# Keeping signed gate peaks and a larger share of finished units in a quantised feed-forward kernel on Trainium2

## The chip, the cores and the metric

The program runs on one core of one Trainium2 chip. The metric is the device time of one execution in microseconds (us), and the runs of one kernel are summed up by their median. Engines are named as in the profile: PE is TensorE, ACT is ScalarE, DVE is VectorE, POOL is GpSimd and SP is SyncE, which here only issues transfers. Each engine works through its own instructions in order; a wait at the head of that queue holds everything behind it.

## What is computed

A cross-attention layer is followed by a feed-forward layer whose every intermediate tensor is rounded to 16-bit integers with one scale for the whole tensor. Only the second part is touched here:

```python
def act_qdq(x):
    qmax = 2.0 ** 15 - 1.0
    scale = jnp.maximum(jnp.max(jnp.abs(x)) / qmax, 1e-12)
    return jnp.clip(jnp.round(x / scale), -qmax - 1.0, qmax) * scale
...
x = act_qdq(x)
up = act_qdq(x @ lpbq_dequant(w_up).T)
gate = act_qdq(x @ lpbq_dequant(w_gate).T)
sig = fixed_qdq_u16(jax.nn.sigmoid(gate))
gate = act_qdq(gate * sig)
o = act_qdq(gate * up)
return o @ lpbq_dequant(w_down).T
```

x has 8192 rows of 512 values, the inner width is 1536. Each act_qdq needs the largest magnitude of its whole tensor before a single value can be rounded. So gate * sig can't be rounded before all of it has been seen once, and o can't be rounded before all products have been seen once.

## The kernel before

The attention part (function opening) ends at 643 us and leaves the normalised rows. The function feed does the rest. It cuts the rows into 16 blocks of 512 and each block's 1536 columns into three units of 128 x 2048 values: 48 units in all (NU). The stages are these.

**Gate pass.** For every block PE multiplies with the gate weights; two halves per unit go from PSUM to a slot of ff_raw (evict, line 1635, ACT). DVE takes the largest magnitude of the unit (raw_peak, line 1417), and POOL stores the unit to DRAM (store_raw, line 1331). ff_raw has three slots. Beside it the up and down weights are quantised.

**Up pass.** PE multiplies the same blocks with the up weights, 48 steps of two halves again; one step is called a stage here, numbered 0 to 47. Each stage takes PE 10.36 us. The block of integers that a PE block needs is loaded by SP (load_hq, line 1206) and split by DVE into two f16 parts (split, line 1406) at the start of every stage 3j+1, for the block that begins with stage 3j+3. While PE works, the gate is finished in two steps.

- A first step (first, lines 1500 and 1655) loads a gate unit, makes its integers, their magnitudes, the sigmoid and its integers, and the largest product of the two. Which units a stage takes is set by first_units (line 1076): 7 in four stages. The integers of all but the last KEPT units are stored to DRAM; those KEPT units stay in SBUF.
- When all 48 largest products are known, a second step (second, lines 1508 and 1667) makes the rounded gate from the integers: a sigmoid on ACT, its integers on DVE, and the product with the scale on DVE. READY units get it, two per stage from stage SECOND = 48 - READY/2 on. In a stage with second steps DVE does the first one, the stage's raw_peak, and the second one, in this order. The first KEPT second steps work on the units that were kept. The rest load their integers again: refill w (load_again, line 1226, SP) brings unit w for second step v = KEPT + w into one of nine slots (AR = 9). The first nine refills find empty slots; a later one waits until the store of the second step that used the slot before has landed. POOL issues that store (store_gated, line 1341) one stage later in its queue, behind the raw store of the stage.

SP's order in the up pass is, for each stage: load_hq if the stage is 3j, the loads of gate units, and from SECOND on a wait for the peak of the stage before and two refills:

```python
for n in range(NU):
    if n % UNITS == 0:
        load_hq(n // UNITS + 1)
    for u in first_units(n):
        load_gate(u + GR)
    if n >= SECOND:
        sp.wait_ge(m["peak"], NU + n - 1)
        load_again(2 * (n - SECOND))
        load_again(2 * (n - SECOND) + 1)
```

**Late stage.** With the scale of the up values known, ACT makes the magnitude of each up unit (line 1720) and DVE the largest product of it with the gate's magnitude (line 1575), 48 places in the order that the tables order, made and home give (lines 952 to 968). PE has nothing to do. A "late" unit, one of the 48 - READY that no second step reached, gets its sigmoid (L1707), integers (L1497), product (L1559) and magnitude (L1727) here. A finished unit needs its magnitude only: on ACT (L1724, "act"), on DVE (L1566 and L1568, "dve"), or already in the up pass (L1681, "done"). Gate units that are not in SBUF are loaded by POOL (load_gated, line 1348), up units by SP (load_up, line 1237). The first loads into the "wq" slots that belong to late units are issued early, in the up pass (soon, line 1359).

**Down stage.** Both factors are loaded once more, multiplied and rounded (last_up, line 1729, ACT; last_product, line 1538, DVE), and PE multiplies with the down weights.

Of the kernel before, what the change touches and what calls it, by code (L numbers as in the profile page):

```python
# [17 lines left out]
P = 128  # L18
# [19 lines left out]
READY = 36  # L38
EARLY = 4
XR = 9  # L40
KEPT = 8
# [870 lines left out]
def feed_memory(s, keep):  # L912
# [8 lines left out]
    for n in ("red_w", "all_w", "unit_w", *(f"{a}_{b}" for a in "gpuo" for b in ("red", "all"))):  # L921
        mem[n] = s.sb(n, [P, 1], F32)
    return mem


def feed(nc, keep, mem, hT_d, hq_d, gate_d, up_d, gate_q, x1_d, out, NB, scale_d, mats):
# [19 lines left out]
    WQ, NEAR = 4, 7  # L946
# [54 lines left out]
    with Scope(nc, "fd") as s:  # L1001
        t_gin, t_ring, t_sig, t_sq, ab, hq, t_h, raw = (mem[n] for n in ("gin", "ring", "sig", "sq", "ab", "hq", "h_parts", "raw"))
# [13 lines left out]
        def floats(t):  # L1016
# [4 lines left out]
        hb = [floats(ab[:, :, :])[:, 0, :], t_gin[:, GR - 1, :]]  # L1021
# [18 lines left out]
                  for n in ("gate_all", "up_all"))  # L1040
# [17 lines left out]
        m = s.sems("g_red g_all p_red p_all u_red u_all o_red o_all dve g_scales u_scales o_scales "  # L1058
                   "hq ah al mm out peak w_peak w_red w_all w_scales w_sent w_q w_real w_hi w_lo "
                   "gq_act gq_dve ab sig sq gpeak g2 mag gp neg ga_late ga_act ga_dve ua prod "  # L1060
                   "fsig fsq fgp fgq fuq fo foq foh fol fmm y")
        gpk, gpk_v, gpk_p = whole_peak(nc, mem, m, "g", keep["gate_peak"][:, :])
# [13 lines left out]
        def first_units(n):  # L1076

            return [u for u in range(NU) if 4 * (u // 7) + u % 7 // 2 == n]
# [9 lines left out]
        def kept(j):  # L1088

            return spare[:, j, :] if j < 6 else more[:, j - 6, :]  # L1090
# [16 lines left out]
        def have_gq(eng, u):  # L1107

            if u % 3 == 0:
                eng.wait_ge(m["gq_act"], u // 3 + 1)  # L1110
            else:
                eng.wait_ge(m["gq_dve"], u - u // 3)
# [26 lines left out]
        def gated(i):  # L1139

            kind, j = g_slot[i][0] if home[i] == "load" else ("unit", order[i])
            if kind == "wq":
                return hq[:, j, :] if j < 2 else ab[:, j - 2, :]
# [37 lines left out]
        with nc.Block() as block:  # L1181
            @block.sync
            def _(sp):
# [30 lines left out]
                def load_gate(u):  # L1214
                    if u < NU:
# [4 lines left out]
                        else:  # L1220
                            have_gq(sp, u - GR)
                            sp.wait_ge(m["ab"], u - GR + 1)
# [3 lines left out]
                def load_again(w):  # L1226
                    if w < AGAIN:
                        if w < AR:
                            sp.wait_ge(m["sig"], NU)
                            sp.wait_ge(m["ab"], NU)  # L1230
# [95 lines left out]
            def _(pool):  # L1326
# [21 lines left out]
                def load_gated(i):  # L1348
# [3 lines left out]
                    if kind == "wq" and prior < 0:  # L1352
                        pool.wait_ge(m["al"], 2 * NB)
                        pool.wait_ge(m["gpeak"], NU)
# [15 lines left out]
                gpk_p(pool)  # L1370
                for n in range(NU):
                    if n == SECOND:
# [30 lines left out]
            def _(dve):  # L1403
# [13 lines left out]
                def raw_peak(n):  # L1417
# [465 lines left out]
```

## Time and profile before

| | us |
|---|---|
| median of 3 runs | 2347.43 |
| lowest and highest run | 2347.32, 2349.02 |
| span of the profiled execution, first to last instruction | 2347.3 |
| attention part | 0 to 643 |
| gate and up pass | 643 to 1644 |
| late stage, with the scales ahead and the first down unit behind it | 1644 to 1837 |
| down stage | 1837 to 2347 |

The page gives the profiled execution's own time as its span; nothing is reported around it. Busy shares of the span are PE 86%, DVE 73%, ACT 60% and POOL 29%, but the stages differ, so they are to be read stage by stage. A busy PE is one that has matmuls in hand. In the rows a line number is that of the kernel before.

### The profile page before, as it was taken

The numbers are of one execution on the slowest core, as the hardware profiler recorded it, in microseconds if no ns is written. First come the engines' busy times: TensorE is split into PE (matmuls) and PEld (weight loads), VectorE is DVE, ScalarE is ACT, GpSimd is POOL, SyncE is SP. The second block draws the span as 40 slices with busy tenths as digits, with TensorE's granted clock in tenths as the row PEclk, the third lists the DMA queues.
The fourth block names the chain that finished last, engine by engine and source line by source line (L and its number), as shares of the span: only waits on it lengthen the run. The fifth ranks groups of instructions, "written<-read, shape, count | busy, mean of one in ns | idle before, by whom it ended". The sixth has DMA issues, their size and how long they took to land.

```text
span 2347.3 us, 25386 instructions
## 1 busy us (share of the span) xinstructions
PE 2020.4 (86%) x9524; PEld 945.0 (40%) x9524; DVE 1715.7 (73%) x1387; ACT 1398.2 (60%) x1599; POOL 670.6 (29%) x662
## 2 busy tenths in 40 slices
PE   5888888888599999999999999999000699999998
PEld 2444444444244444444444444444000344444443
DVE  8799999999634534532499998999899644577641
ACT  4678887887422322322499996676899633366530
POOL 2599999998300000000121110222111000000000
PEclk9999999999799999999999999999555899999999
DMA  7789999998346656743699995787998755555541
GB/s 297 283 314 337 348 337 346 335 350 316 126 181 226 225 207 223 259 148 144 242 378 390 378 369 209 264 320 293 401 419 327 291 229 208 205 201 232 233 152 72
DMA packets 131162, 634.60 MB, mean 270 GB/s; under 512 B 12256, under 2 KB 12768, under 8 KB 91104
## 3 DMA queue, kind: packets, MB, share of 16 engines
q1 hardware_dynamic: 85888, 316.81, 37.0%
q0 software_dynamic: 45152, 316.16, 34.6%
q8 instruction: 76, 1.25, 0.2%
q14 instruction: 46, 0.38, 0.0%
HBM read 430.69 MB, written 202.24 MB: 270 GB/s over the span
## 4 chain that ended last, share of the span: by engine, by line
PE 64%; issue 3%; DVE 3%; ACT 2%; POOL 0%; DVEq 0%; ACTq 0%; POOLq 0%
PE fd_pp L1777 42%; PE fd_pp L1791 21%; ACT ff_ring L1720 1%; DVE ff_sig L1575 1%; DVE ff_h_parts L1559 1%; DVE ff_sq L1497 1%; ACT ff_sig L1707 0%; DVE ff_sq L1566 0%; DVE kept_gate L1568 0%; DVE ff_gin L1510 0%; DVE ff_hq L1549 0%; ACT ff_hq L1632 0%; ACT ff_ring L1746 0%; ACT ff_sig L1736 0%; DVE kept_o_peak L1575 0%
## 5 line engine op out<-in xcount | busy, mean ns | idle before, releaser
L1791 PE MATMUL fd_pp<-ff_down,kept_gate 128*128 128x512 f16 x1536 | 458.9, 381 | 193.1 <-DVE ff_up L1616 193.1
L1777 PE MATMUL fd_pp<-ff_h_parts,kept_gate 128*128 128x512 f16 x2304 | 499.6, 380 | 14.3 <-DVE ff_h_parts L1415 14.3
L1777 PE MATMUL fd_pp<-ff_h_parts,ff_up 128*128 128x512 f16 x2304 | 497.4, 379 | 0.0
L1639 ACT ACTIVATE ff_raw<-fd_pp 128x1024 f32<-128x1024 f32 x192 | 194.3, 1017 | 396.5 <-PE fd_pp L1777 396.5
L1777 PEld LDWEIGHTS fd_pp<-ff_h_parts,kept_gate 128*128 128x128 f16 x2304 | 225.9, 98 | 287.9 <-DVE ff_h_parts L1415 14.7
L1777 PEld LDWEIGHTS fd_pp<-ff_h_parts,ff_up 128*128 128x128 f16 x2304 | 225.4, 98 | 271.8
L1420 DVE TENSOR_REDUCE kept_gate_peak<-ff_raw 128x1 f32<-128x2048 f32 x48 | 109.7, 2285 | 292.9 <-ACT ff_raw L1639 292.9
L1791 PEld LDWEIGHTS fd_pp<-ff_down,kept_gate 128*128 128x128 f16 x1536 | 150.6, 98 | 375.9 <-issue 195.8
L1791 PE MATMUL fd_pp<-ff_down,ff_up 128*128 128x512 f16 x768 | 292.2, 380 | 0.0
L1746 ACT ACTIVATE ff_ring<-ff_hq,kept_g 128x2048 int16<-128x2048 f32 x48 | 96.0, 1999 | 191.1 <-DVE ff_hq L1549 189.7
L790 PE MATMUL at_psO<-kept_wo,at_ahi 128*128 128x512 f16 x512 | 155.5, 386 | 36.2 <-ACT at_alo L277 31.6
L1614 DVE CAST kept_gate<-ff_ring 128x2048 f16<-128x2048 int16 x48 | 33.3, 693 | 180.1 <-PE fd_pp L1791 136.7
L790 PE MATMUL at_psQ<-kept_wq,at_xhi 128*128 128x512 f16 x512 | 155.5, 386 | 4.8 <-ACT at_xlo L268 1.6
L1334 POOL DMA_DIRECT2D gate_scratch<-ff_raw x48 | 26.5, 553 | 463.3 <-DVE kept_gate_peak L1420 463.3
L697 POOL TENSOR_TENSOR at_kv_rows<-at_kv_rows 128x1024 f32<-128x1024 f32 x62 | 146.8, 2368 | 4.9
L515 DVE TENSOR_TENSOR at_kv_rows<-at_kv_rows,at_psQ 128x2048 f32<-128x2048 f32 x64 | 143.3, 2279 | 4.4 <-PE at_psQ L790 4.4
L1394 POOL DMA_DIRECT2D out<-ff_h_parts x15 | 12.5, 834 | 467.3 <-DVE ff_h_parts L1592 440.0
L520 DVE TENSOR_REDUCE at_sc<-at_kv_rows 128x64 f32<-128x2048 f32 x64 | 143.0, 2274 | 0.0
L1497 DVE TENSOR_SCALAR ff_sq<-ff_sig 128x2048 uint16<-128x2048 f32 x96 | 117.3, 1222 | 9.8 <-ACT ff_sig L1665 6.0
L1420 DVE TENSOR_REDUCE kept_up_peak<-ff_raw 128x1 f32<-128x2048 f32 x48 | 109.5, 2282 | 18.3 <-ACT ff_raw L1639 17.9
L1334 POOL DMA_DIRECT2D up_scratch<-ff_raw x48 | 41.2, 859 | 249.0 <-DVE kept_up_peak L1420 249.0
L1791 PEld LDWEIGHTS fd_pp<-ff_down,ff_up 128*128 128x128 f16 x768 | 75.4, 98 | 91.4 <-issue 1.4
(239 smaller groups left out, 3454.9 us busy)
## 6 DMA issues: line engine op xcount, KB each, us to landing
ff_raw<-up_scratch SPq DMA_DIRECT2D x66, 1024.0 KB, 8.5
gate_scratch<-ff_raw POOLq DMA_DIRECT2D x48, 1024.0 KB, 9.1
ff_gin<-gate_scratch SPq DMA_DIRECT2D x48, 1024.0 KB, 8.7
up_scratch<-ff_raw POOLq DMA_DIRECT2D x48, 1024.0 KB, 7.7
ff_gin<-gate_integers SPq DMA_DIRECT2D x73, 512.0 KB, 5.8
gate_integers<-ff_ring POOLq DMA_DIRECT2D x43, 512.0 KB, 8.7
ff_up<-up_scratch SPq DMA_DIRECT2D x21, 1024.0 KB, 9.5
kept_xs<-in_x SPq DMA_DIRECT2D x32, 512.0 KB, 14.6
```

The costliest lines, as they stand in the source:

```text
L515: nc.vector.tensor_tensor(keys, keys, psQ[t % 2][:, :].unsqueeze(1).to_broadcast([P, W, D]), ALU.mult).then_inc(m["prod"], 1)
L520: nc.vector.tensor_reduce(raw[:, t % 2], kv[:, t % KR, :, 0:D].rearrange("p w (h e) -> p w h e", h=H), AX.X, ALU.add).then_inc(m["raw"], 1)
L697: nc.gpsimd.tensor_tensor(lower, lower, upper, ALU.add).then_inc(m["half"], 1)
L790: mm = nc.tensor.matmul(out[:, :], a[:, slot, c, :], w[b][:, c, :], start=(q == 0), stop=(q == len(todo) - 1))
L1334: pool.dma_start(to[n // UNITS, n % UNITS], raw[:, n % UNITS, :]).then_inc(stored[n % UNITS], 16)
L1420: nc.vector.tensor_reduce(keep[to][:, k:k + 1], raw[:, n % UNITS, :], AX.X, ALU.max, apply_absolute_value=True).then_inc(m["peak"], 1)
L1497: nc.vector.tensor_scalar(sq[:, :], sig[:, a, :], 65536.0, 65535.0, ALU.mult, ALU.min).then_inc(m["sq"], 1)
L1614: nc.vector.tensor_copy(piece(oh, k), fo_oq).then_inc(m["foh"], 1)
L1639: nc.scalar.activation(raw[:, n % UNITS, h * 2 * BLK:(h + 1) * 2 * BLK], pp[(2 * n + h) % 4][:, :, :].rearrange("p a t -> p (a t)"), ACT.C ...
L1746: nc.scalar.activation(fo_oq, fo_o, ACT.Copy, scale=g[:, 13:14]).then_inc(m["foq"], 1)
L1777: mm = nc.tensor.matmul(pp[k % 4][:, h, :], wt[w][:, c, f:f + P], a[:, b % 2, :, c, :], start=(q == 0), stop=(q == len(todo) - 1))
L1791: mm = nc.tensor.matmul(pp[k % 8 // 2][:, k % 2, :], a[b % 2][:, f, t * P:(t + 1) * P], wt[w][:, f, :], start=(q == 0 and i == 0), stop=(q ...
```

## The change

READY goes from 36 to 42 and KEPT from 8 to 10, so that SECOND moves from stage 30 to 27, and AWAY, the first kept unit, from 40 to 38. The two kept units more lie in two slots added to ring; the buffer ab is gone.

In the gate pass DVE takes each unit's maximum and minimum in place of its largest magnitude; the last unit of the gate pass and of the up pass is reduced in two halves. The scales of the gate are used negated, so the gate integers are negated, and the largest product of a first step is taken from the signed integers (the negative gates, whose negated integers are positive); the positive side is covered by one value, the product at the largest gate, made once from a 128 x 1 column. The first step's magnitude on ACT and the integers on DVE go away: ACT makes all integers. A slot of ring is now free for a new unit when the first step's largest product is taken, where it was the sigmoid. First steps run 15 in eight stages, where it was 7 in four. SP's first refills wait for the end of the first steps, and POOL's early list has two slots to look at in place of four. ACT's first two conversions of the down stage (last_up) wait for the last use of the two kept slots that they write, and no longer for every kept slot from there on.

```diff
-READY = 36
+READY = 42
...
-KEPT = 8
+KEPT = 10
...
-    mem = {"gin": s.sb("gin", [P, 4, UE], F32), "ring": s.sb("ring", [P, 4, UE], I16),
+    mem = {"gin": s.sb("gin", [P, 4, UE], F32), "ring": s.sb("ring", [P, 6, UE], I16),
...
-           "ab": s.sb("ab", [P, 2, UE], I16), "hq": s.sb("hq", [P, 2, DC * BLK], I16),
+           "hq": s.sb("hq", [P, 2, DC * BLK], I16),
...
-    WQ, NEAR = 4, 7
+    WQ, NEAR = 2, 7
...
-            return [u for u in range(NU) if 4 * (u // 7) + u % 7 // 2 == n]
+            return [u for u in range(NU) if u // 15 * 8 + u % 15 * 8 // 15 == n]
...
-            return spare[:, j, :] if j < 6 else more[:, j - 6, :]
+            return spare[:, j, :] if j < 6 else more[:, j - 6, :] if j < 8 else ring[:, QR + j - 8, :]
...
-                eng.wait_ge(m["sig"], u - QR + 1)
+                eng.wait_ge(m["gpeak"], u - QR + 1)
...
-                    if n == SECOND:
+                    if n == SECOND - 1:
                         ppk_p(pool)
...
-                def raw_peak(n):
-                    dve.wait_ge(m["out"], 2 * n + 2)
-                    to, k = ("gate_peak", n) if n < NU else ("up_peak", n - NU)
-                    nc.vector.tensor_reduce(keep[to][:, k:k + 1], raw[:, n % UNITS, :], AX.X, ALU.max,
-                                            apply_absolute_value=True).then_inc(m["peak"], 1)
...
+                def gate_range(n):
+                    for h in halves(n):
+                        values, k = part(n, h), n + h
+                        nc.vector.tensor_reduce(keep["gate_top"][:, k:k + 1], values, AX.X, ALU.max)
+                        last = nc.vector.tensor_reduce(keep["gate_low"][:, k:k + 1], values, AX.X, ALU.min)
+                    last.then_inc(m["peak"], 1)
+
+                def up_range(n):
+                    for h in halves(NU + n):
+                        values, k = part(NU + n, h), n + h
+                        last = nc.vector.tensor_reduce(keep["up_peak"][:, k:k + 1], values, AX.X, ALU.max, apply_absolute_value=True)
+                    last.then_inc(m["peak"], 1)
...
                 def first(u):
                     sigmoid_integer(u, u % 2)
-                    gate_integers(u + 2)
-                    dve.wait_ge(m["ab"], u + 1)
-                    nc.vector.tensor_tensor_reduce(out=sig[:, u % 2, :], in0=ab[:, u % 2, :], in1=sq[:, :], scale=1.0,
+                    nc.vector.tensor_tensor_reduce(out=sig[:, u % 2, :], in0=integers(u), in1=sq[:, :], scale=1.0,
...
-                    if u % 3 == 0:
-                        gq_free(act, u)
-                        if u >= AWAY:
-                            act.wait_ge(m["mm"], NB * PAIRS)
-                        nc.scalar.activation(integers(u), gin[:, u % GR, :], ACT.Copy, scale=g[:, 5:6]).then_inc(m["gq_act"], 1)
+                    gq_free(act, u)
+                    if u >= AWAY:
+                        act.wait_ge(m["mm"], NB * PAIRS)
+                    nc.scalar.activation(integers(u), gin[:, u % GR, :], ACT.Copy, scale=g[:, 5:6]).then_inc(m["gq"], 1)
                     need(act, m["gpeak"], u - 1)
-                    nc.scalar.activation(ab[:, u % 2, :], gin[:, u % GR, :], ACT.Abs, scale=g[:, 5:6]).then_inc(m["ab"], 1)
...
-                            act.wait_ge(m["prod"], max(g_last["unit", u] for u in range(AWAY + 6, NU)) + 1)
+                            act.wait_ge(m["prod"], max(g_last["unit", u] for u in range(AWAY + 6, AWAY + 8)) + 1)
```

Two places show how instructions stand against each other. The first is DVE's queue before the split of stage 43 (L1413 or L1417, the CAST from ff_hq). L1510 or L1538 is the end of a second step, L1497 or L1527 its sigmoid integers, L1420 or L1442 the peak of a stage. Before, from second step 22, the first one of stage 41:

```order
L1510 SCALAR_TENSOR_TENSOR ff_gin<-ff_sq,kept_g,ff_gin 128x2048
L1420 TENSOR_REDUCE kept_up_peak<-ff_raw 128x1
L1497 TENSOR_SCALAR ff_sq<-ff_sig 128x2048
L1510 SCALAR_TENSOR_TENSOR ff_gin<-ff_sq,kept_g,ff_gin 128x2048
L1497 TENSOR_SCALAR ff_sq<-ff_sig 128x2048
L1510 SCALAR_TENSOR_TENSOR ff_gin<-ff_sq,kept_g,ff_gin 128x2048
L1420 TENSOR_REDUCE kept_up_peak<-ff_raw 128x1
L1497 TENSOR_SCALAR ff_sq<-ff_sig 128x2048
L1510 SCALAR_TENSOR_TENSOR ff_ring<-ff_sq,kept_g,ff_ring 128x2048
L1413 CAST ff_h_parts<-ff_hq 128x2048
L1415 TENSOR_TENSOR ff_h_parts<-ff_hq,ff_h_parts 128x2048
```

Those were second steps 22 to 25. Now, from second step 30, the first one of stage 42:

```order
L1538 SCALAR_TENSOR_TENSOR ff_gin<-ff_sq,kept_g,ff_gin 128x2048
L1442 TENSOR_REDUCE ff_up_peak<-ff_raw 128x1
L1527 TENSOR_SCALAR ff_sq<-ff_sig 128x2048
L1538 SCALAR_TENSOR_TENSOR ff_gin<-ff_sq,kept_g,ff_gin 128x2048
L1417 CAST ff_h_parts<-ff_hq 128x2048
L1419 TENSOR_TENSOR ff_h_parts<-ff_hq,ff_h_parts 128x2048
```

The split follows the second steps of stage 42 in both; steps 30 and 31 stand where 24 and 25 stood.

The second place is SP's queue at stages 39 to 42: six refills and the load of integers that the split of stage 43 needs. Each refill waits for the semaphore of its slot, w mod 9; the names are those of an earlier scope (at_q_lo is slot 0, at_scaled 1, at_turned 2, at_taken 3, at_rest 4, at_out 5, at_kv_ready 6, at_kv_out 7, at_consts 8), and at_sqe or at_hT_sb is the peak of the stage before. Before, refills 18 to 23:

```order
L1235 DMA ff_gin<-gate_integers 128x2048 [waits at_q_lo,at_sqe]
L1235 DMA ff_gin<-gate_integers 128x2048 [waits at_scaled]
L1235 DMA ff_gin<-gate_integers 128x2048 [waits at_turned,at_sqe]
L1235 DMA ff_gin<-gate_integers 128x2048 [waits at_taken]
L1235 DMA ff_gin<-gate_integers 128x2048 [waits at_rest,at_sqe]
L1235 DMA ff_gin<-gate_integers 128x2048 [waits at_out]
L1212 DMA ff_hq<-h_integers 128x2048 [waits at_ssq_v]
```

Now, refills 24 to 29:

```order
L1239 DMA ff_gin<-gate_integers 128x2048 [waits at_kv_ready,at_hT_sb]
L1239 DMA ff_gin<-gate_integers 128x2048 [waits at_kv_out]
L1239 DMA ff_ring<-gate_integers 128x2048 [waits at_consts,at_hT_sb]
L1239 DMA ff_gin<-gate_integers 128x2048 [waits at_q_lo]
L1239 DMA ff_gin<-gate_integers 128x2048 [waits at_scaled,at_hT_sb]
L1239 DMA ff_gin<-gate_integers 128x2048 [waits at_turned]
L1217 DMA ff_hq<-h_integers 128x2048 [waits at_x_ssq]
```

The load of integers still follows the second refill of stage 41; that refill is number 29 now, and waits for slot 2, where it was number 23 and slot 5.

## Rows read from the trace of the kernel before

**Rows 1.** Stretches: length, busy PE, PEld, DVE, ACT, POOL, PE clock, DMA share, GB/s.

```profile
642.00:1145.00 503.00, 498.14 (x2299) 225.40 (x2300) 197.29 (x121) 138.29 (x119) 35.26 (x65) 0.99 0.58 202
1460.00:1644.00 184.00, 183.71 (x852) 83.08 (x849) 171.98 (x102) 122.07 (x83) 44.05 (x54) 1.00 0.78 291
1643.80:1836.80 193.00, 0.00 (x0) 0.00 (x1) 175.41 (x156) 177.09 (x94) 20.46 (x34) 0.51 0.92 373
```

**Rows 2.** The chain of waits, in order of time: start, length, engine, tile, line.

```profile
646.86 996.86 PE fd_pp L1777 x4608
...
1836.83 497.62 PE fd_pp L1791 x2292
```

**Rows 3.** Stretches: the late stage from its first magnitude to its last product.

```profile
1652.80:1827.30 174.50, 0.00 (x0) 0.00 (x0) 163.23 (x136) 162.79 (x86) 17.38 (x28) 0.50 0.94 384
```

**Rows 4.** Instructions by form, one form of each line: total busy us, mean ns.

```profile
L1724 ACT ACTIVATE kept_gate<-kept_gate 128x2048 int16<-128x2048 int16 x5 | 9.5, 1894 | 0.0
...
L1559 DVE TENSOR_TENSOR ff_h_parts<-ff_sig,ff_sq 128x2048 f32<-128x2048 int16 x3 | 6.9, 2293 | 0.1
...
L1727 ACT ACTIVATE ff_hq<-ff_h_parts,kept_g 128x2048 int16<-128x2048 f32 x3 | 6.0, 2002 | 2.6 <-DVE ff_h_parts L1559 2.6
...
L1707 ACT ACTIVATE ff_sig<-ff_hq,kept_g 128x2048 f32<-128x2048 int16 x3 | 6.0, 1992 | 0.0
...
L1568 DVE TENSOR_TENSOR ff_gin<-ff_gin,ff_sq 128x2048 int16<-128x2048 int16 x3 | 3.7, 1225 | 0.1
```

**Rows 5.** DVE in order of time, stages 41 to 44 of the up pass.

```profile
1582.64 2.29 DVE L1420 TENSOR_REDUCE kept_up_peak<-ff_raw 128x1 f32<-128x2048 f32 x1
...
1593.00 2.29 DVE L1420 TENSOR_REDUCE kept_up_peak<-ff_raw 128x1 f32<-128x2048 f32 x1 [0.84 <-ACT ff_raw L1639]
1595.20 1.22 DVE L1497 TENSOR_SCALAR ff_sq<-ff_sig 128x2048 uint16<-128x2048 f32 x1
...
1598.73 0.69 DVE L1413 CAST ff_h_parts<-ff_hq 128x2048 f16<-128x2048 int16 x1
...
1604.11 2.28 DVE L1420 TENSOR_REDUCE kept_up_peak<-ff_raw 128x1 f32<-128x2048 f32 x1
...
1613.72 2.29 DVE L1420 TENSOR_REDUCE kept_up_peak<-ff_raw 128x1 f32<-128x2048 f32 x1
```

**Rows 6.** POOL in order of time, its stores after the peak of stage 41.

```profile
1585.22 0.96 POOL L1334 DMA_DIRECT2D up_scratch<-ff_raw  x1 [4.94 <-DVE kept_up_peak L1420]
1586.17 0.53 POOL L1346 DMA_DIRECT2D gate_integers<-ff_gin  x1
```

**Rows 7.** SP in order of time, the second refill of stage 41 and load_hq.

```profile
1591.61 0.32 SPq L1235 DMA_DIRECT2D ff_gin<-gate_integers  x1
1591.97 0.44 SPq L1212 DMA_DIRECT2D ff_hq<-h_integers  x1
```

**Rows 8.** Lines L1212 (load_hq, 3) and L1346 (store_gated, 17), 1500 to 1600 us.

```profile
DMA to landing us min/median/max: 4.3/4.5/4.6
...
DMA to landing us min/median/max: 3.9/5.2/6.7
```

**Rows 9.** All engines in order of time, the end of the late stage.

```profile
1827.37 3.89 ACT L1736 ACTIVATE ff_sig<-ff_raw,kept_g 128x2048 int16<-128x2048 f32 x2 [4.89 <-DVE kept_o_peak L1575]
...
1829.40 2.29 DVE L1549 TENSOR_TENSOR ff_hq<-ff_gin,ff_sig 128x2048 f32<-128x2048 int16 x1 [1.89 <-ACT ff_sig L1736]
1831.61 0.21 DVE L905 TENSOR_SCALAR kept_g<-ff_o_all,kept_g 128x1 f32<-128x1 f32 x1
```

**Rows 10.** DMA issues of the late stage, gate loads: count, KB, median us to landing.

```profile
kept_gate<-gate_integers POOLq DMA_DIRECT2D x10, 512.0 KB, 8.6
```

**Rows 11.** Stretches: the late stage's first part, and the up pass's first part.

```profile
1652.80:1750.00 97.20, 0.00 (x0) 0.00 (x0) 91.37 (x75) 91.55 (x49) 10.70 (x17) 0.50 1.01 418
1230.00:1260.00 30.00, 30.00 (x140) 13.62 (x139) 29.58 (x24) 28.41 (x19) 4.82 (x8) 1.00 1.01 406
1200.00:1400.00 200.00, 200.00 (x928) 90.69 (x927) 196.97 (x156) 182.70 (x116) 36.54 (x50) 1.00 0.98 380
```

More of the change, by code:

```diff
@@ L916, in feed_memory @@
         keep[n] = [keep[n + "_all"][:, i] for i in range(2)]
[L917 removed]
+    mem = {"gin": s.sb("gin", [P, 4, UE], F32), "ring": s.sb("ring", [P, 6, UE], I16),
            "sig": s.sb("sig", [P, 3, UE], F32), "sq": s.sb("sq", [P, UE], U16),
[L919 removed]
+           "hq": s.sb("hq", [P, 2, DC * BLK], I16),
            "h_parts": s.sb("h_parts", [P, 2, 2, SUB, DC, P], F16), "raw": s.sb("raw", [P, UNITS, UE], F32)}
[L921 removed]
+    for n in ("red_w", "all_w", "unit_w", *(f"{a}_{b}" for a in "puo" for b in ("red", "all"))):
         mem[n] = s.sb(n, [P, 1], F32)
+    for n in ("g_red", "g_all"):
+        mem[n] = s.sb(n, [P, 2], F32)
+    for n in ("gate_top", "gate_low", "up_peak", "gated_peak"):
+        keep[n] = s.sb(n, [P, count + 1], F32)
+    keep["o_peak"] = s.sb("o_peak", [P, count], F32)
+    mem["top_sig"] = s.sb("top_sig", [P, 1], F32)
+    mem["top_int"], mem["top_sq"] = s.sb("top_int", [P, 1], I16), s.sb("top_sq", [P, 1], U16)
     return mem
@@ L1001, in feed @@
     with Scope(nc, "fd") as s:
-        t_gin, t_ring, t_sig, t_sq, ab, hq, t_h, raw = (mem[n] for n in ("gin", "ring", "sig", "sq", "ab", "hq", "h_parts", "raw"))
+        t_gin, t_ring, t_sig, t_sq, hq, t_h, raw = (mem[n] for n in ("gin", "ring", "sig", "sq", "hq", "h_parts", "raw"))
+        top_sig, top_int, top_sq = (mem[n] for n in ("top_sig", "top_int", "top_sq"))
         red, allm, unit = (mem[n] for n in ("red_w", "all_w", "unit_w"))
@@ L1415, in split, with halves, part @@
                     nc.vector.tensor_tensor(lo, hq[:, b % 2, :], hi, ALU.subtract).then_inc(m["al"], 1)
-                def raw_peak(n):
-                    dve.wait_ge(m["out"], 2 * n + 2)
-                    to, k = ("gate_peak", n) if n < NU else ("up_peak", n - NU)
-                    nc.vector.tensor_reduce(keep[to][:, k:k + 1], raw[:, n % UNITS, :], AX.X, ALU.max,
-                                            apply_absolute_value=True).then_inc(m["peak"], 1)
+                def halves(n):
+                    return (0, 1) if n % NU == NU - 1 else (0,)
+                def part(n, h):
+                    if n % NU < NU - 1:
+                        dve.wait_ge(m["out"], 2 * n + 2)
+                        return raw[:, n % UNITS, :]
+                    dve.wait_ge(m["out"], 2 * n + h + 1)
+                    return raw[:, n % UNITS, h * 2 * BLK:(h + 1) * 2 * BLK]
+                def gate_range(n):
[9 more added lines that the diff above has]
+                    last.then_inc(m["peak"], 1)
                 def weight_peak(i, h):
@@ new lines, in top_product @@
+                def top_product():
+                    dve.wait_ge(m["top_s"], 1)
+                    nc.vector.tensor_scalar(top_sq[:, :], top_sig[:, :], 65536.0, 65535.0, ALU.mult, ALU.min).then_inc(m["top_q"], 1)
+                    dve.wait_ge(m["top_q"], 1)
+                    nc.vector.scalar_tensor_tensor(out=keep["gated_peak"][:, NU:NU + 1], in0=top_int[:, :], scalar=-1.0,
+                                                   in1=top_sq[:, :], op0=ALU.mult, op1=ALU.mult).then_inc(m["top_p"], 1)
```

68 lines of the change are left out of this document (35 added, 33 removed).

## The prediction

> **What bounds the kernel now.** I read the profile by stretches first. In the gate pass and the up pass TensorE (PE) works without a gap: the chain of waits is one PE piece of 996.9 us, and the down stage is another of 497.6 us [rows 2]. Between them lies the late stage, 193 us in which PE does nothing while ScalarE (ACT) and VectorE (DVE) finish the 12 units that the up pass left over and form all 48 products [rows 1]. From the first magnitude to the last product it is 174.5 us, ACT busy for 162.8 and DVE for 163.2 [rows 3]; their records overlap the next one a little, so both queues are full. So there are two ways to change the time: the late stage is paid in full, and in the up pass nothing costs until DVE or ACT falls behind PE. DVE is near that: in the second part of the up pass it is busy for 172.0 of 184 us [rows 1].
>
> **Late stage: -18 us.** Late units go from 12 to 6; finished units whose magnitude ACT takes here go from 15 to 18, those where DVE takes it from 8 to 9 (the table that lines 952 to 968 of the kernel before make, worked out with the new numbers). A late unit costs ACT a sigmoid of 1.99 us and a magnitude of 2.00, and DVE an integer step of 1.22 and a product of 2.29; an ACT magnitude of a finished unit is 1.89 and DVE's pair for one is 1.23 plus a shorter negation [rows 4, 5]. ACT: 6 x 3.99 - 3 x 1.89 = 18.3 us less. DVE: 6 x 3.51 = 21.1 less, and about 1.9 more for the pair: 19.2. I take 18. The upper bound is 20, both queues with some idle time gone. The lower bound is 14: two early gate loads vanish (with two "wq" slots, both first users are finished units, so the list of early loads is empty), and the first late unit, at place 7, is now loaded only after the first product. Such a load took 8.6 us to land, in the median of ten [rows 10]; issued some 4.4 us into the stage it lands at 13, where ACT wants it after four magnitudes, at 7.6; DVE has four products to form meanwhile, so of these 5.4 us at most 4 are lost.
>
> **Tail of the late stage: -1.9 us.** The first down-stage factor (last_up(0)) waited for the last product: ACT idle 4.89 us, then 1.99 us, and DVE's 2.29 us behind it before the last quantiser [rows 9]. Now it waits for place 38 and is made long before. DVE's multiply follows the last product at once, its 2.29 us still cover POOL's reduction, and the quantiser starts 1.9 us earlier. Bounds 0 and 1.9.
>
> **Up pass, second part: +28 us.** This is the term that decides. A second step v may write its result over a slot of nine, and SP refills that slot when the store of the earlier occupant has landed. The refill w waits for the store of second step v = KEPT + w - 9. That was w - 1; with KEPT = 10 it is w + 1. SP's second refill of stage 41 was w = 23 and waited for v = 22, the first second step of stage 41; now it is w = 29 and waits for v = 30, the first one of stage 42. SP is in order, and right behind that refill stands the load of the next integer block (load_hq), which DVE's split at the start of stage 43 needs.
>
> The trace has the whole chain, one stage earlier. DVE starts the peak of stage 41 at 1582.64 [rows 5]; POOL issues the raw store at 1585.22 and only then the store of v = 22, at 1586.17 [rows 6]; that has landed at 1591.61, when SP refills, and SP issues load_hq at 1591.97 [rows 7]: 9.33 us from the start of the peak. The load takes 4.5 us [rows 8]: 13.83. DVE reaches the split 5.73 us after the start of the peak of stage 42 (1593.00 to 1598.73) [rows 5]. Today the load lands at about 1596.5, 2.3 us ahead. After the change the same chain hangs on the peak of stage 42 itself, so the split starts 13.83 us after it instead of 5.73: DVE stands still for 8.1 us, with every later peak and second step queued behind it.
>
> It happens wherever SP ends a stage 3j-1 with such a refill (w of 9 and more, up to 31): before the splits of stages 34, 37, 40 and 43, four times. Nothing of DVE's work can fill the hole, since the queue is in order. Of slack there is little: a stage with a split takes DVE 11.11 us when it runs without waits (1593.00 to 1604.11), one without 9.61 (to 1613.72), so three take 30.33 against 3 x 10.36 = 31.08 of PE: 0.75 us per block, and 0.75 per stage in the last two. So 4 x (8.1 - 0.75) - 1.5 = 27.9 us later at the end of the pass. PE waits for the splits too: the last one ends 13.83 + 1.86 us after the start of a peak that is by then 3 x 7.35 us late, 1593.0 + 22.1 + 15.7 = 1630.8, where PE would begin its last block at 1643.7 - 31.1 = 1612.6 [rows 2]. That is 18 us, of which the two blocks before take 3 and 7; but DVE is later still, so the pass ends by DVE. The peak of the last stage in two halves would give up to 1.1 us if DVE were waiting there; it isn't any more, so 0.
>
> For the store and the load the Trainium skill (DMA: Bandwidth & Descriptors, Anatomy of one DMA) has a fit of about 2.0 us plus bytes over 436 GB/s, 3.2 us for such a half MB. By that the chain would be 7.1 + 3.2 us, the hole 4.6 and the term +14, and the sum would be a gain of 6 us. The trace disagrees: the store took 5.4 us here, 5.2 in the median, 3.9 at the least, and the load 4.3 to 4.6 [rows 8]. I go by the trace. Its ends: 3.9 and 4.3 make 7.8 + 4.3 = 12.1, a hole of 6.4 and a term of 21; 6.7 and 4.6 make 15.2, 9.5 and 33.5.
>
> **Costed at nothing.** Gate pass: a minimum beside each maximum, 48 x 2.29 = 110 us more on DVE, which was busy for 197 of 503 us there [rows 1]; so 306 us were idle. Where weight work falls into the same stage and the two don't fit into 10.36 us, the slot of ff_raw comes free later; there are three, and the cost stays 0 while the delay is under two stages, 20 us. First part of the up pass: ACT loses 48 magnitudes and takes over DVE's 32 conversions, so both have less to do; DVE was the tight one there, 29.6 of 30 us [rows 11]. Both are hidden by PE; only the earlier end of the part counts, and the new table of first units spends it. The extra one-column steps between the passes, five or six of 0.2 us, are covered by the missing magnitude of the first unit, some 2 us of ACT like its others [rows 4], and by the three pairs that PE may run ahead, 15.5 us.
>
> **Sum.** The profiled execution has a span of 2347.3 us, the median of the runs is 2347.43: the same within 0.1. 2347.3 + 27.9 - 18.0 - 1.9 = **2355.3 us**, slower by 0.34%. A change of under 0.2%, 4.7 us, is what a measurement can't tell from none.
>
> **Rivals.**
> **No hole: 2327.4 us.** If load_hq is issued within 1.2 us of the start of the stage's peak, it lands before DVE's split and only -18 - 1.9 is left. For it: today's split never waits there, and the integers are loaded a whole block ahead on paper. Against it: the load that SP issues at 1591.97 follows a store that POOL can't issue before the peak [rows 6, 7], and I find no other path. It decides where the chain is under 5.73 us; break-even with the savings is at a hole of 6.1 us. Chance 0.13.
> **Quick landings: 2346.4 us, no change.** While DVE stands still fewer transfers are under way, and all four stores and loads land as fast as the fastest row: +21 - 20 - 1.9 = -0.9. Against it: the 17 stores and 3 loads of that stretch lie about their medians although the DMA engines are not full there. Chance 0.08. The fit of the Trainium skill, above, lies beyond it.
> **DMA full in the first part: about 2364 us.** 15 first units in 8 stages need 15 x 1.57 + 8 x 1.05 + 2.7 x 0.52 = 33.4 MB in 82.9 us, 403 GB/s, where 14 needed 384. The stretch moved 380 on average at a share of 0.98, and 406 in one of 30 us [rows 11]. If 380 were the limit, the part would run 5 us late per 8 stages for 20 stages, 12.5 us, of which PE's lead hides some 4: 8 us on top. Against it: the late stage moved 418 GB/s for 97 us [rows 11]. Chance 0.07. The Trainium skill (DMA: Bandwidth & Descriptors, Specifications) gives 358 GB/s of HBM per core, by which even the present part could not run; that trace row decides against it.
>
> **Chances and range.** Forecast with its bounds 0.72, the rivals 0.13, 0.08, 0.07. The forecast's ends: +21.1 - 20 - 1.9 = 2346.5 and +33.5 - 14 = 2366.8. The range 2345 to 2367 leaves out the first rival and a little at the top. Faster by over 0.2%: the first rival and a bit of the second, 0.14. Within: the rest of the second and the low end of the forecast, 0.12. Slower: 0.74.
>
> **What would show it.** DVE's CAST of the split (L1417) waits for the DMA of ff_hq four times, some 8 us each, from stage 34 on; PE has three gaps in the up pass, about 18 us together; the first magnitude of the late stage starts at about 1681 instead of 1652.8; the late stage has 6 late products and takes about 156 us from first magnitude to last product; the first last_up of ACT starts before the last product. Wrong if that CAST does not wait, if PE's up pass has no gap, or if gaps lie before stage 27.

## The result, and the profile after

The changed kernel takes 2369.81 us (median of 4 runs, 2368.63 to 2371.02); the kernel before, on the same chip, 2348.22 us. The ratio is 1.0093, with a 95% interval of 1.0080 to 1.0105: **slower by 21.6 us**. The prediction was 2355.3 us, slower by 8, in a range of 2345 to 2367. The sign and the mechanism of the loss were right; the size was not, and the measured time lies above the range. Two terms carry the miss, the saving in the late stage above all.

The span of the profiled execution is 2369.2 us, where it was 2347.3. The stretches of the changed kernel that answer to [rows 1, 3], with the same columns (length, busy PE, PEld, DVE, ACT, POOL, PE clock, DMA share, GB/s):

```profile
642.00:1145.00 503.00, 497.94 (x2298) 225.36 (x2299) 302.63 (x170) 137.71 (x119) 35.28 (x65) 0.99 0.57 201
1460.00:1676.00 216.00, 190.27 (x852) 84.34 (x850) 172.94 (x100) 127.53 (x86) 44.15 (x54) 0.96 0.65 244
1685.60:1720.00 34.40, 0.00 (x0) 0.00 (x0) 22.11 (x19) 24.44 (x13) 2.11 (x4) 0.50 1.00 399
1720.00:1790.00 70.00, 0.00 (x0) 0.00 (x0) 64.91 (x57) 64.10 (x35) 7.74 (x13) 0.50 1.01 417
1685.60:1852.40 166.80, 0.00 (x0) 0.00 (x0) 144.37 (x126) 149.96 (x80) 15.57 (x27) 0.50 0.97 397
```

The gate pass carries its 105 us of extra DVE work beside an unchanged PE. The second part of the up pass has the same DVE work as before, 172.9 us, in a longer time. The late stage has less work (ACT 150.0 us where it was 162.8), but takes 166.8 us, and in its first 34 us neither engine is busy for more than 24.4.

The chain of waits answers to [rows 2]. Its first piece of PE now ends at 1514, and the holes follow: stretches in which DVE stands still ahead of a split, because the block of integers has not landed. The PE piece, and the chain at the second of the four holes (start, length, what):

```profile
647.06 867.34 PE fd_pp L1810 x4008
...
1538.76 2.21 DVE ff_up_peak L1442
1540.97 0.28 issue
1541.25 0.95 POOL up_scratch L1338
1542.20 6.28 DMA gate_integers<-ff_ring
1548.50 0.32 SPq L1239
...
1548.86 5.15 DMA ff_hq<-h_integers
1554.03 0.70 DVE ff_h_parts L1417
```

This is the chain of the prediction, link by link: peak, POOL's raw store, the landing of the second step's store, SP's refill, the block load, the split. It takes 15.27 us from the start of the peak where 13.83 were predicted. The splits of DVE and the gaps of PE, each in order of time, with the wait ahead in brackets:

```profile
1514.41 0.69 DVE L1417 CAST ff_h_parts<-ff_hq 128x2048 f16<-128x2048 int16 x1 [8.67 <-PE fd_pp L1810]
...
1554.03 0.69 DVE L1417 CAST ff_h_parts<-ff_hq 128x2048 f16<-128x2048 int16 x1 [9.55 <-DMA ff_hq<-h_integers]
...
1594.23 0.69 DVE L1417 CAST ff_h_parts<-ff_hq 128x2048 f16<-128x2048 int16 x1 [10.13 <-DMA ff_hq<-h_integers]
```

```profile
1556.04 32.83 PE L1810 MATMUL fd_pp<-ff_h_parts,ff_up 128*128 128x512 f16 x144 [5.40 <-DVE ff_h_parts L1419]
1596.24 33.20 PE L1810 MATMUL fd_pp<-ff_h_parts,ff_up 128*128 128x512 f16 x144 [7.37 <-DVE ff_h_parts L1419]
1636.42 33.59 PE L1810 MATMUL fd_pp<-ff_h_parts,ff_up 128*128 128x512 f16 x144 [6.97 <-DVE ff_h_parts L1419]
```

The first hole is put down to PE, since the split also waits for matmuls; but its block load was issued at 1509.1 and such loads took 5.1 to 5.4 us here, so it landed when the split began. (In the kernel with the early gate loads, below, whose up pass has the same order, the same hole is put down to the block load.) The list of waits for 1400 to 1680 us gives the other three 29.8 us together:

```profile
DVE ff_h_parts L1417 <- DMA ff_hq<-h_integers: 29.8, 3, 10.1
PE fd_pp L1810 <- DVE ff_h_parts L1419: 19.7, 3, 7.4
```

So there are four holes of 38.5 us in all, where 32.4 were predicted, and three gaps of PE, 19.7 us, where 18 were. The start of the late stage, ACT and POOL in order of time:

```profile
1685.63 5.79 ACT L1753 ACTIVATE ff_ring<-ff_raw,kept_g 128x2048 int16<-128x2048 f32 x3 [7.50 <-DVE kept_g L1567]
...
1690.36 0.53 POOL L1360 DMA_DIRECT2D ff_ring<-gate_integers  x1 [4.77 <-DVE ff_o_peak L1607]
...
1695.34 1.91 ACT L1757 ACTIVATE ff_hq<-ff_hq 128x2048 int16<-128x2048 int16 x1 [2.03 <-DMA ff_hq<-gate_integers]
...
1702.73 2.00 ACT L1740 ACTIVATE ff_sig<-ff_ring,kept_g 128x2048 f32<-128x2048 int16 x1 [5.48 <-DMA ff_ring<-gate_integers]
...
1706.65 2.29 DVE L1607 CUSTOM_DVE_ANT_0 ff_sig<-ff_hq,ff_ring 128x2048 bf16<-128x2048 int16 x1 [9.96 <-ACT ff_ring L1753]
```

The gate load of the first late unit (place 7) is issued at 1690.36, after the first product, and ACT can go on at 1702.73: 12.4 us. ACT waits 5.5 us for it, and DVE 10 us behind ACT.

The end of the late stage answers to [rows 9]:

```profile
1849.60 3.88 ACT L1769 ACTIVATE ff_sig<-ff_raw,kept_g 128x2048 int16<-128x2048 f32 x2
...
1850.11 2.29 DVE L1607 CUSTOM_DVE_ANT_0 ff_sig<-ff_ring 128x2048 bf16<-128x2048 int16 x1
...
1852.55 2.28 DVE L1581 TENSOR_TENSOR ff_hq<-ff_gin,ff_sig 128x2048 f32<-128x2048 int16 x1
...
1860.30 1.01 PE L1824 MATMUL fd_pp<-ff_down,kept_gate 128*128 128x512 f16 x2 [190.29 <-DVE ff_up L1648]
```

Where the time went: the first magnitude starts at 1685.63 where it was 1652.82, **+32.8**; from there to the end of the last product 166.8 where it was 174.5, **-7.7**; from there to PE 7.9 where it was 9.6, **-1.7**; the down stage **-1.6**. That is the 21.9 us between the spans. The last of these is not explained by the change: over the ten kernels of this document the down stage takes 508.9 to 510.5 us.

### The profile page after: what moved, and what is told of

It reads as the page before. It is cut to its first block, busy times and chain, and to the rows that moved or that the text cites. A ratio compares the mean times of both kernels' runs of the same rounds, so it can differ in the third digit from the quotient of the medians.

```text
span 2369.2 us, 25333 instructions
## 1 busy us (share of the span) xinstructions
PE 2025.4 (85%) x9524; PEld 945.8 (40%) x9524; DVE 1765.6 (75%) x1404; ACT 1348.9 (57%) x1571; POOL 663.4 (28%) x664
## 4 chain that ended last, share of the span: by engine, by line
PE 58%; DVE 6%; DMA 4%; issue 3%; ACT 2%; POOL 0%; SPq 0%; DVEq 0%; ACTq 0%; POOLq 0%
PE fd_pp L1810 37%; PE fd_pp L1824 21%; DVE ff_gin L1538 2%; DVE ff_sq L1527 1%; ACT ff_ring L1753 1%; DMA gate_integers<-ff_gin 1%; DMA ff_ring<-gate_integers 1%; DMA ff_hq<-h_integers 1%; DVE ff_sig L1607 1%; DVE ff_up_peak L1442 0%; DMA kept_gate<-gate_integers 0%; DMA ff_hq<-gate_integers 0%; DVE ff_ring L1538 0%; DVE ff_h_parts L1591 0%; DMA gate_integers<-ff_ring 0%
## 5 line engine op out<-in xcount | busy, mean ns | idle before, releaser
L1810 PE MATMUL fd_pp<-ff_h_parts,ff_up 128*128 128x512 f16 x2304 | 503.8, 382 | 19.7 <-DVE ff_h_parts L1419 19.7
L1435 DVE TENSOR_REDUCE ff_gate_top<-ff_raw 128x1 f32<-128x2048 f32 (+1 forms) x49 | 109.9, 2242 | 187.7 <-ACT ff_raw L1671 187.7
L1527 DVE TENSOR_SCALAR ff_sq<-ff_sig 128x2048 uint16<-128x2048 f32 x96 | 117.3, 1222 | 21.9 <-ACT ff_sig L1695 19.1
L1442 DVE TENSOR_REDUCE ff_up_peak<-ff_raw 128x1 f32<-128x2048 f32 (+1 forms) x49 | 109.6, 2237 | 16.1 <-ACT ff_raw L1671 15.9
L525 DVE TENSOR_TENSOR at_kv_rows<-at_kv_rows,at_pr 128x1536 f32<-128x1536 f32 x64 | 109.8, 1755 | 1.1
```

The costliest lines, as they stand in the source:

```text
L525: nc.vector.tensor_tensor(values, values, pr[:, t % 2, 0:W - 1].unsqueeze(3).to_broadcast([P, W - 1, H, HD]), ALU.mult).then_inc(m["pv"], 1)
L1435: nc.vector.tensor_reduce(keep["gate_top"][:, k:k + 1], values, AX.X, ALU.max)
L1442: last = nc.vector.tensor_reduce(keep["up_peak"][:, k:k + 1], values, AX.X, ALU.max, apply_absolute_value=True)
L1527: nc.vector.tensor_scalar(sq[:, :], sig[:, a, :], 65536.0, 65535.0, ALU.mult, ALU.min).then_inc(m["sq"], 1)
L1810: mm = nc.tensor.matmul(pp[k % 4][:, h, :], wt[w][:, c, f:f + P], a[:, b % 2, :, c, :], start=(q == 0), stop=(q == len(todo) - 1))
```

## The experiments

Theory 1: the holes come from the integer load that stands in SP's queue behind a refill, which waits for a second step two later than before. Rival: four more second steps are too much for DVE. Theory A: the late stage gives back its gain because the first late unit's gate load is no longer early. Theory B: it gives it back because its bytes are the bound. The kernel before was run again beside each group of experiments, 2348.08 us beside the first four below and 2348.48 beside the other four; the ratios are to these.

**The block load ahead of the refills.**

```
-                    if n % UNITS == 0:
-                        load_hq(n // UNITS + 1)
+                    if n % UNITS == 2:
+                        load_hq(n // UNITS + 2)
```

(Block 1 is loaded ahead of the loop.)

> The change, but SP issues the load of an integer block one stage earlier, ahead of the two refills of stage 3j-1 and no longer behind them. Theory (the refill that waits for the first second step of the stage holds the block load up): DVE's CAST of the split no longer waits for the load, PE's three gaps in the up pass (5.4, 7.4, 7.0 us) are gone, and the late stage's first magnitude starts at about 1653 in place of 1685.6. The late stage itself stays at some 167 us. Time 2369.8 - 32.8 = about 2337. Rival (42 second steps are by themselves more than DVE can do beside PE): the CAST doesn't wait, but peaks and second steps run late by themselves; the first magnitude stays behind 1670 and the time above 2354.

Measured: 2343.11 us, ratio to the kernel before 0.9978 (0.9969 to 0.9988). PE has no gap in the up pass any more, and the first magnitude starts at 1652.56, 33.1 us earlier:

```profile
1399.82 244.49 PE L1811 MATMUL fd_pp<-ff_h_parts,ff_up 128*128 128x512 f16 x1132
...
1652.56 5.79 ACT L1754 ACTIVATE ff_ring<-ff_raw,kept_g 128x2048 int16<-128x2048 f32 x3 [3.60 <-DVE kept_g L1568]
...
1667.59 1.91 ACT L1758 ACTIVATE ff_hq<-ff_hq 128x2048 int16<-128x2048 int16 x1 [7.35 <-DMA ff_hq<-gate_integers]
1675.14 2.00 ACT L1741 ACTIVATE ff_sig<-ff_ring,kept_g 128x2048 f32<-128x2048 int16 x1 [5.63 <-DMA ff_ring<-gate_integers]
```

For the up pass theory 1 holds to half a microsecond, and the rival falls. The time is 6 us above the expected one, since some of the 33 are lost again: the late stage takes 171.4 us in place of 166.8. The gate loads that POOL issues at 1651.38 and 1657.29 now run beside the first up loads, which SP began to issue at 1644.46; ACT gets them at 1667.59 and 1675.14, 16 and 18 us after their issue. In the changed kernel the holes had held DVE back: the first gate load followed the first up load by 14 us (1670.17 to 1684.45), where it is 7 us here. That this makes the difference was not tried by itself.

**The wait alone, in the kernel before.**

```
-                    if n % UNITS == 0:
+                    if n < SECOND and n % UNITS == 0:
                         load_hq(n // UNITS + 1)
...
                         load_again(2 * (n - SECOND) + 1)
+                    if n >= SECOND and n % UNITS == 0:
+                        load_hq(n // UNITS + 1)
```

> The kernel before with one part of the change's timing alone: from stage 30 on, the load of an integer block stands behind the two refills of stage 3j, one stage later than before, so that it hangs on the first second step of that stage as in the changed kernel. Theory: three holes on DVE ahead of the splits of stages 37, 40 and 43 (refills wait only from number 9 on and end with number 27), each about 9.9 us as measured in the changed kernel, less 0.75 us of slack per block and 1.5 us at the end: 3 x 9.15 - 1.5 = 26 us, time about 2374. With the 8.1 us of the prediction it would be 20.5, about 2369. Rival (the loss comes from the larger number of second steps): under 5 us, below 2353.

Measured: 2371.27 us, ratio 1.0097 (1.0080 to 1.0114), 23.2 us more than before. The three splits:

```profile
1545.68 0.69 DVE L1415 CAST ff_h_parts<-ff_hq 128x2048 f16<-128x2048 int16 x1 [8.66 <-PE fd_pp L1779]
1586.32 0.69 DVE L1415 CAST ff_h_parts<-ff_hq 128x2048 f16<-128x2048 int16 x1 [10.58 <-DMA ff_hq<-h_integers]
1624.66 0.69 DVE L1415 CAST ff_h_parts<-ff_hq 128x2048 f16<-128x2048 int16 x1 [8.28 <-DMA ff_hq<-h_integers]
```

27.5 us of holes less 3 x 0.75 and 1.5 us of slack are 23.8; the first magnitude is 23.0 us later (1675.82). The block load moved by two places in SP's queue, with nothing else of the change, costs as much as the whole change.

**The store of the second step ahead of the raw store.**

```
+                    for v in second_units(n - 1)[:1]:
+                        store_gated(v)
                     if n >= 1:
                         store_raw(NU + n - 1)
-                    for v in second_units(n - 1):
+                    for v in second_units(n - 1)[1:]:
                         store_gated(v)
```

> The change, but POOL stores the result of a stage's first second step ahead of the stage's raw store; the order of loads stays. Theory (the hole is a chain from the peak through POOL's raw store, the store of the second step, the refill and the block load): the chain starts when the second step ends, not when the peak has ended and the raw store is issued, which is 2.29 + 0.29 + 0.95 = 3.5 us earlier, so each of the four holes is about 3.5 us shorter: 14 us in all, about 2356. If the store also lands faster because no 1 MB store stands in front of it in POOL's queue (4 us in place of 6.3 to 6.6), up to 6 us each: 24 us, about 2346. Rival (the DMA engines are the limit there and the landing moves with the traffic): less than 5 us, above 2365.

Measured: 2358.27 us, ratio 1.0039 (1.0025 to 1.0053), 11.5 us less than the change, somewhat short of the 14 that the theory gave for the earlier start alone. The holes are 6.60, 6.62, 5.89 and 7.57 us, 26.7 in all. The chain of waits at the second one, to be compared with the one above:

```profile
1535.94 0.28 issue
1536.22 2.94 DMA gate_integers<-ff_ring
1539.17 0.32 SPq L1239
1539.53 8.71 DMA ff_hq<-h_integers
1548.27 0.70 DVE ff_h_parts L1419
```

The store now lands in 2.94 us where it took 6.28, and the load takes 8.71 us where it took 5.15: 11.65 and 11.43 together. What one gained the other lost, and the 1 MB raw store that stood ahead of the store is now issued at 1538.41, 1.1 us ahead of the load. The other three holes give 3.84 and 8.70, 3.03 and 7.87, 3.60 and 8.98, together 10.9 to 12.6; the other two whole chains of the change, 6.59 and 5.42, 6.65 and 5.33, give 12.0 each. Only the earlier start of the chain is left, about 3 us per hole.

For a half MB store the Trainium skill's fit (DMA: Bandwidth & Descriptors, Anatomy of one DMA — SWDGE (gpsimd) path), which is for transfers issued by POOL, gives an estimate of 3.2 us. The store that has nothing right ahead of it in POOL's queue, at 2.94 to 3.84 us here, comes near that, and the same store behind the raw store in the changed kernel, at 6.28 to 6.65, doesn't.

**The gate load of the first late unit early.**

```
-    g_slot, g_last = assign({**{("wq", j): -1 for j in range(WQ)}, **residents}, loaded)
+    soon = [loaded[0], made.index("late")]
+    g_slot, g_last = assign({**{("wq", j): -1 for j in range(WQ)}, **residents}, soon + [i for i in loaded if i not in soon])
...
-                soon = [i for i in loaded[:WQ] if late(order[i])]
```

> The change, but the two slots for early gate loads go to places 4 and 7 (the first late unit) in place of 4 and 6, and both loads are issued in the up pass at stage 46. Theory A (the late stage's start is lost because the first late unit's gate load is issued only after the first product): ACT's first late sigmoid no longer waits 5.5 us for its load nor DVE 10 us behind it; the late stage takes 158 to 161 us in place of 166.8, time about 2362 to 2364. Theory B (the late stage is bound by its bytes, 66.2 MB at 418 GB/s): only the 1 MB that moves ahead of the stage is saved, 2.5 us, about 2367.

Measured: 2363.56 us, ratio 1.0071 (1.0054 to 1.0088), 6.3 us less than the change. Neither wait at the start is there any more, and the late stage takes 161.7 us, 5.1 less. That is near theory A's 158 to 161; but with two gate loads issued ahead the stage also moves fewer bytes, 65.3 MB where it moved 66.2, and by theory B 2.2 of the 5.1 us could be theirs. The two shares were not separated, and 161.7 is not yet the 156 of the prediction.

The order of the up pass up to stage 46 is that of the change, and its splits show how much the holes vary from one execution to another:

```profile
1513.93 0.69 DVE L1417 CAST ff_h_parts<-ff_hq 128x2048 f16<-128x2048 int16 x1 [8.47 <-DMA ff_hq<-h_integers]
...
1553.24 0.69 DVE L1417 CAST ff_h_parts<-ff_hq 128x2048 f16<-128x2048 int16 x1 [9.24 <-DMA ff_hq<-h_integers]
...
1591.67 0.69 DVE L1417 CAST ff_h_parts<-ff_hq 128x2048 f16<-128x2048 int16 x1 [8.38 <-DMA ff_hq<-h_integers]
...
1630.35 0.69 DVE L1417 CAST ff_h_parts<-ff_hq 128x2048 f16<-128x2048 int16 x1 [8.62 <-DMA ff_hq<-h_integers]
...
1681.56 5.79 ACT L1753 ACTIVATE ff_ring<-ff_raw,kept_g 128x2048 int16<-128x2048 f32 x3 [7.50 <-DVE kept_g L1567]
```

They make 34.7 us where the change had 38.5, and the first magnitude starts 28.7 us later than in the kernel before, not 32.8. In the chains the store takes 5.44 to 6.42 us and the load 4.42 to 5.05, together 10.3 to 11.1. So 4.1 of the 8.1 us between the two spans lie in the up pass, where the edit does nothing before stage 46; why is not shown.

**Both repairs.** The edits are those of the first and the fourth kernel above.

> The change with both repairs: the block load ahead of the refills, and the gate loads of places 4 and 7 issued in the up pass. Theory (two independent losses): first magnitude at about 1652.6 as with the first repair alone, and of the 13 us (7.4 and 5.6) that ACT then waited for gate loads at the start of the late stage some 8 to 10 go; time about 2333 to 2335. The load of place 6 is still issued only after the first product and may hold DVE for up to 4 us: then 2337. Rival (the late stage is bound by its bytes): 2.5 us saved, 2340.6.

Measured: **2330.74 us**, ratio 0.9924 (0.9908 to 0.9941): the fastest kernel here that loads everything, 17.7 us under the kernel before and 39 under the change, and 2 us under what was expected. The first magnitude starts at 1651.19, the late stage takes 162.0 us.

**Both repairs, with fewer bytes.** Every second place of the late stage loads half of its up unit, so that part of the largest product is taken of stale values.

```
+                    w = UE // 2 if i % 2 else UE
-                    sp.dma_start(u_slot(i), up_d[u // UNITS, u % UNITS])...
+                    sp.dma_start(u_slot(i)[:, 0:w], up_d[u // UNITS, u % UNITS][:, 0:w])...
```

> As the kernel with both repairs, but of the up units that the late stage loads from DRAM every second place loads only half of its columns, so that the largest product there is taken of partly stale values; some 11 of 66 MB are left out and no work of ACT or DVE. Theory B (with the early loads in place, what keeps the late stage at 162 us is its bytes, 66 MB at 418 GB/s = 158 us, where ACT is busy for 151): the late stage falls to 152 to 155 us and the time by 7 to 10 us against the kernel with both repairs. Rival (the order of ACT and DVE and their waits for each other set it): the late stage stays above 159 us, less than 3 us saved.

Measured: 2326.91 us, ratio 0.9910 (0.9894 to 0.9927), 3.8 us less than with both repairs, where 7 to 10 were expected. In the profiled executions the spans differ by 5.2 us, and the late stage takes 155.8 us where it took 162.0, just above the 152 to 155 that theory B gave. Its stretches, first with all bytes, then with fewer:

```profile
1652.50:1687.00 34.50, 0.00 (x0) 0.00 (x0) 30.99 (x27) 30.91 (x17) 3.73 (x7) 0.50 1.01 421
1687.00:1722.00 35.00, 0.00 (x0) 0.00 (x0) 29.96 (x28) 30.44 (x17) 3.07 (x5) 0.50 1.02 419
1722.00:1757.00 35.00, 0.00 (x0) 0.00 (x0) 33.39 (x28) 33.04 (x18) 3.60 (x6) 0.50 1.02 420
1757.00:1792.00 35.00, 0.00 (x0) 0.00 (x0) 31.87 (x31) 34.75 (x20) 5.18 (x9) 0.50 1.02 418
```

```profile
1687.00:1722.00 35.00, 0.00 (x0) 0.00 (x0) 32.77 (x29) 31.89 (x17) 3.53 (x6) 0.50 0.93 350
1722.00:1757.00 35.00, 0.00 (x0) 0.00 (x0) 34.20 (x32) 34.71 (x19) 4.27 (x8) 0.50 0.90 343
1757.00:1792.00 35.00, 0.00 (x0) 0.00 (x0) 32.39 (x29) 34.75 (x20) 4.52 (x8) 0.50 0.85 333
```

The list of waits agrees: with all bytes ACT waits four times for a late unit's gate load, 7 us in all; with fewer once, 0.2 us. So the bytes do hold the stage up, but by less than theory B gave: 4 us by the medians and 6 by the two traces. With all bytes the rows show 418 to 421 GB/s at a share of 1.01 to 1.02 while ACT and DVE are not full.

**KEPT back at 8.** The only edit is `KEPT = 8`; still 42 finished units.

> The change with KEPT back at 8 alone: 42 finished units, 34 refills, and refill w waits for the store of second step w-1 as before the change. SP's order is the changed kernel's. Theory (the hole comes from the two kept units more, which let each refill wait for a second step two later): DVE's CAST of the split doesn't wait for its load, PE has no gap, and the first magnitude starts at about 1653; the late stage is that of the first repair alone (171 us, no early gate load of a late unit) with two gate loads more, 1 MB, 2.5 us: about 2343 to 2346. Rival (the four second steps more in the up pass, by themselves, make the hole): it stays, about 2366 to 2372.

Measured: 2347.78 us, ratio 0.9999 (0.9989 to 1.0008). No split waits for its load, and the first magnitude starts at 1650.45, earlier than before: the holes came with the two kept units more, not with the second steps. The late stage, though, takes 176.5 us, 2.0 more than in the kernel before, with half its late units, and the time is 2 us above the expected range. ACT waits 7.56 and 5.64 us for gate loads at its start, as with the block load moved:

```profile
1665.69 1.91 ACT L1757 ACTIVATE ff_hq<-ff_hq 128x2048 int16<-128x2048 int16 x1 [7.56 <-DMA ff_hq<-gate_integers]
1673.23 2.00 ACT L1740 ACTIVATE ff_sig<-ff_sig,kept_g 128x2048 f32<-128x2048 int16 x1 [5.64 <-DMA ff_sig<-gate_integers]
```

**KEPT back at 8, three early gate loads.** One of the two slots that this frees becomes a third "wq" slot, and the loads of places 4, 6 and 7 are issued in the up pass.

```
-    WQ, NEAR = 2, 7
+    WQ, NEAR = 3, 7
-                return hq[:, j, :]
+                return hq[:, j, :] if j < 2 else ring[:, QR, :]
-                soon = [i for i in loaded[:WQ] if late(order[i])]
+                soon = loaded[:WQ]
```

> KEPT back at 8 as in the run before, and the slot that this frees is a third one for early gate loads: those of places 4, 6 and 7 are issued in the up pass. Theory: no hole and no wait for gate loads at the start of the late stage, which takes 159 to 163 us: about 2331 to 2335, the fastest of all. Rival (bytes): 3 loads fewer in the late stage, 1.5 MB, 3.8 us under the run with KEPT at 8 alone.

Measured: 2337.25 us, ratio 0.9953 (0.9937 to 0.9970), 2 us above the expected range and not the fastest. The waits at the start are gone, and the late stage takes 166.3 us, 10 less than with KEPT at 8 alone, but 4 more than with both repairs. Against both repairs two gate loads more are needed and one more is early, so the stage moves 66.7 MB where it moved 66.2, 1.3 us at 418 GB/s; what the rest is was not tried.

## Why the prediction was right in sign and wrong in size

**Second part of the up pass: +27.9 predicted, +32.8 measured.** Mechanism, number of holes, their places and the arithmetic held: each hole is the chain less 5.73 us (15.27 - 5.73 = 9.54; 9.55 in the row), and 38.5 less 4 x 0.75 and 1.5 are 34.0. What was too small is the chain's 13.83 us, in which the store has 5.4 and the load 4.5: in the three chains that the trace of the change shows whole, the store took 6.28, 6.59 and 6.65 and the load 5.15, 5.42 and 5.33. The bounds, 21 to 33.5, held it.

Two things bear on the size of this miss. The trace before had this chain three times, at 9.5, 10.3 and 9.3 us from the start of the peak to the issue of the block load, and the prediction took the shortest; the longest is

```profile
1551.56 2.29 DVE L1420 TENSOR_REDUCE kept_up_peak<-ff_raw 128x1 f32<-128x2048 f32 x1
...
1561.88 0.57 SPq L1212 DMA_DIRECT2D ff_hq<-h_integers  x1
```

And the kernel with the early gate loads shows +28.7 with the same order, so the size is not known better than to some 4 us. The kernel with the store first shows that the two landings trade against each other at about the same sum, so the sum is the thing to price; it was 9.9 us in the prediction and 10.2 to 12.5 in the nine whole chains of the three kernels with this order. Why it came out longer is not shown. The fit of the Trainium skill that the prediction tried on both transfers is one for transfers issued by POOL, as said above; the block load is issued by SP, and none here landed in less than 4.4 us.

**Late stage: -18 predicted, -7.7 measured.** This is the step that put the time outside the range: with the 14 us of its lower bound the rest would have come out at about 2363. Its count of the work was right in the instructions, 6 late units and 18 and 9 magnitudes of finished ones. ACT's busy time in the stretch fell by 12.8 us all the same, and not by 18.3, since one of the twelve sigmoids of before had run ahead of the stretch (at 1648.32), and the first two down-stage conversions now stand at its end (at 1849.60); DVE's fell by 18.9, where 19.2 were counted. With fewer bytes the stage takes 155.8 us, 18.7 less than before, where 156 was forecast; that agreement takes both repairs and the missing bytes.

Two things were left out of the price. First, up to 5.1 us (166.8 against 161.7): the prediction saw that the first late unit's gate load would be issued after the first product, and capped the loss at "at most 4" with a landing of 8.6 us, the median of ten [rows 10]. It took 12.4, with up loads of 1 MB under way around it, and DVE stood still for 10 us. With the block load moved the same kind of load took 16 and 18 us, and the loss was 9.4 (171.4 against 162.0). Of the two differences 2.2 and 2.6 us can be the bytes that left the stage with the early loads (0.9 and 1.1 MB at 418 GB/s). Second, some 4 to 6 us of bytes, which the sum put at nothing: "both queues are full" was taken to mean that only ACT and DVE bound the stage. The stretch itself [rows 3] showed a DMA share of 0.94 at 384 GB/s beside them, and [rows 11] 418 GB/s. The list of transfers gave 67.0 MB for the stage before and gives 66.2 after: at 418 GB/s that is 160 and 158 us, below the 174.5 of then and above the 156 that was forecast. As ACT and DVE got less to do, the bytes became a bound beside them.

**Tail: -1.9 predicted, -1.7 measured.** Held; DVE's product follows at once, and ACT's first last_up stands ahead of the last product.

**Costed at nothing.** Held: PE has no gap before the one that ends at 1556 us, with 105 us more DVE work in the gate pass and 15 first steps in eight stages.

**Rivals.** The hole was there; the landings inside the chain were not quick but slower than their medians; the first part of the up pass shows no gap, so the DMA engines did not bound it.

## What to carry to other kernels

When a change alters how many buffers rotate, write down for every in-order queue which earlier store each transfer now waits for, and what stands behind it: here two slots more moved a wait by two steps and an unrelated load paid for it, which one moved line repaired. When a stage is shortened, compare the new time with the bytes of the stage over the rate that it already reaches, not only with its engines. Price the first transfers of a stage as they land with everything else that starts there, not at the median of the whole stage.

## What the runs showed of the hardware

A half MB store issued about 1 us behind a 1 MB store, and the half MB load that waited for it, took 10.2 to 12.5 us together (6.28 and 5.15, 6.59 and 5.42, 6.65 and 5.33 in the change; 5.44 to 6.42 and 4.42 to 5.05 with the early gate loads; 7.74 and 4.71, 5.68 and 4.47 in the kernel before with the wait alone). With the store first and the 1 MB store issued 1 to 2 us ahead of the load, the two took 10.9 to 12.6 us (2.94 to 3.84 and 7.87 to 8.98). A gate load of 512 KB took 12.4 to 18 us to be usable when 1 MB loads were issued around it, where the median of ten in the late stage before was 8.6. With both repairs the core moved 418 to 421 GB/s in each of four stretches that make up 139.5 us.
